# Scaling of one weight split over the two ends of a two-layer attention kernel, and idle matrix products on TensorE in its last batch and last feed-forward

## The chip, the cores and the metric

The kernel runs on one core of a Trainium2 chip. The metric is the device time of one execution in microseconds (us). The engines are TensorE (PE in the profile; PEld are its weight loads), VectorE (DVE), ScalarE (ACT), GpSimd (POOL) and the queue that SyncE (SP) feeds with transfers.

## The reference, cut to what matters

Two layers run over 32 batches of 112 rows with 256 columns; each batch has a context of 375 rows.

```python
x = x + xattn0(layernorm(x), ctx)   # 16 heads of 64
x = x + ffn0(layernorm(x))          # ternary weights, rows quantised to 8 bits, conv over rows, silu
x = x + xattn1(layernorm(x), ctx)   # 16 heads of 16, RMS norm and rotary on q and k
x = x + ffn1(layernorm(x))          # w1, w2 quantised per row; inputs by ONE scale over all batches

def quant_weight_int8_perchannel(w):          # used by ffn1
    s = maximum(max(abs(w), axis=1, keepdims=True), EPS) / 127.0
    return clip(round(w / s), -128.0, 127.0) * s
def quant_act_uint8(x):                       # the maximum is over the whole tensor
    s = maximum(max(x), EPS) / 255.0
    return clip(round(x / s), 0.0, 255.0) * s
```

Since ffn1 takes a maximum over all batches, it can only start when the last batch has left xattn1. A second such maximum, over the hidden values, stands between its two halves.

## The kernel before, in words

**Order.** It is written out by hand for each engine, with semaphores between the engines. All engines run: an opening (weights, batch 0's keys, values and queries, and the first 8 head pairs, `attention(OPENING)`), then a loop of 31 rounds, each `rest(b)` and `attention(MIDDLE, b)`, then `rest(31, True)` and `attention(CLOSING, 31)`, and then ffn1 over 8 groups of 4 batches.

**`rest`.** It ends the first attention of batch b (`wo0_product`, L471), takes the row statistics (`moments`), quantises the rows to `xq` (L1065), turns them on PE (L540), multiplies (L550), runs the convolution on DVE and ACT (L1173, L1185, L854), turns the result (L563), quantises it (L1209, L1210), turns it (L574), multiplies (L588), adds it (L1220), normalises it (L1006), turns it (L597), forms the queries of xattn1 (L605), rotates them on DVE (L1232 to L1239) and turns them (`query_turn`, L478). In a loop round PE works on the next batch's keys and values between these steps (`k0_proj`, `v0_proj`, L339). In the last batch there is no next batch, and nothing stands between them.

**`scales(n, part)`.** This scales the weights of ffn1 on DVE. Weight 0 (`f1w1`, 128x2048 numbers) lies in `stage[1]`, weight 1 in `stage[0]`. Part 0 takes the row maxima and their reciprocals (L1139, L1140, L1142), part 1 multiplies (L1144), part 2 rounds into `wnat[n]` (L1147), which lies in the memory of xattn0's query and output weights and so has to wait for the last batch. Weight 0's three parts stand at the head of `rest(31)`, ahead of the sum `x1` (L1161) in DVE's order. `stage[1]` is free, and `f1w1` is loaded into it, since early in the opening (an issue of SP at 33.4 us).

**`ctx_lo`** (L1449) is POOL's subtraction that gives the low part `cT_lo` of the next batch's context; PE needs it for the third and later products of the next batch's keys. POOL does rotary steps (L1476 to L1482) and the inverse roots of the row statistics (L1444, L1445) in the same queue.

**ffn1.** PE turns the weights (L666), waits for their copies, spreads the global maximum (L670, L672), turns the first rows (L688), and makes the hidden values (L679), of which DVE takes the maxima (L1366). Then the second maximum is spread (L704, L706), the hidden values are made again (L679), ACT applies the ReLU (L968), and the second product follows (L721).

Of the kernel before, what the change touches and what calls it, by code (L numbers as in the profile page):

```python
# [10 lines left out]
ALU = mybir.AluOpType  # L11
# [3 lines left out]
P = 128  # L15
# [37 lines left out]
def xattn_ffn_kernel(nc, A, x3_dram, out):  # L53
# [24 lines left out]
    with ExitStack() as ctx:  # L78
# [254 lines left out]
        def _(pe):  # L333
# [191 lines left out]
            def rest(b, last_batch):  # L525
# [8 lines left out]
                if not last_batch:  # L534
                    k0_terms(0, 4).then_inc(s["k0_ready"], 1)
                    k0_proj(b + 1, range(1, 5), True)

                pe.wait_ge(s["xq_ready"], b + 1)
                for c in range(DC):
                    last = pe.transpose(pt_b0[:, c * T:(c + 1) * T], xq[:, c * P:(c + 1) * P], identb[0:T, 0:T])  # L540
# [13 lines left out]
                if not last_batch:  # L554
                    k0_terms(5, 3).then_inc(s["k0_ready"], 1)
                    k0_proj(b + 1, [6, 7], True)
                    v0_proj(b + 1, [0, 1])
                    pe.wait_ge(s["k0_sb"], b * IC + (IC + 7))
                    v0_terms(2, 0, 4)
                for j in range(FC):  # L560
                    if j % HT == 0:
                        pe.wait_ge(s["y_ready"], b * 2 + (j // HT + 1))
                    last = pe.transpose(pa[0:T, j // HT, (j % HT) * P:(j % HT + 1) * P], th[:, j, :], ident[:])  # L563
                    if j % HT == HT - 1:
                        last.then_inc(s["yT_ready"], 1)
                if not last_batch:
                    x0_transpose(b + 1)
                    v0_terms(2, 4).then_inc(s["v0_ready"], 1)
                    q0_proj(b + 1, 0)
                    q0_proj(b + 1, 1, range(0, 1))  # L570
                for j in range(FC):
                    if j % HT == 0:
                        pe.wait_ge(s["hq_ready"], b * 2 + (j // HT + 1))
                    last = pe.transpose((pt_b0, pt_b1)[j // HT][:, (j % HT) * T:(j % HT + 1) * T],  # L574
                                        hq[:, j * P:(j + 1) * P], identb[0:T, 0:T])
                    if j % HT == HT - 1:
                        last.then_inc(s["hqT_ready"], 1)
# [12 lines left out]
                if not last_batch:  # L590
                    v0_proj(b + 1, [3])
                    q0_proj(b + 1, 1, range(1, HT))
                    v0_terms(4, 0, 2)

                pe.wait_ge(s["xn2_ready"], b + 1)
                for c in range(DC):
# [10 lines left out]
                if not last_batch:  # L607
# [2 lines left out]
                    pe.wait_ge(s["q0_sb"], b * 2 + 4)  # L610
                    scores(1, MIDDLE, b)
                else:
                    query_turn(b)
                    pe.wait_ge(s["x3_ready"], b + 1)
                    pe.wait_ge(s["q1_sb"], b + 1)
                    for i in range(AHEAD):
                        scores(i, CLOSING, b)

            def weight_sum(n):

# [50 lines left out]
            pe.wait_ge(s["g_used"], 2)  # L671
            pe.matmul(pt[:, 1, 0:1], ones[0:1, :], t8[0:1, 1, 0:1], start=True, stop=True).then_inc(s["g_ready"], 1)  # L672
            pe.wait_ge(s["wT_sb"], 4)

            def hidden(c, i, dst):

# [16 lines left out]
            for c in range(NCH):  # L693
                pe.wait_ge(s["xq3T_sb"], c + 2)
                for i in range(4):
# [4 lines left out]
                    if i == 2 and c < NCH - 1:  # L700
                        transpose_rows(c + 1)

            pe.wait_ge(s["g_used"], 3)
            pe.transpose(pt[0:1, 0, 0:P], t8[:, 2, 0:1], ident[:]).then_inc(s["g_ready"], 1)  # L704
            pe.wait_ge(s["g_used"], 4)
# [275 lines left out]
        def _(dve):  # L981
# [105 lines left out]
            def x3_step(n, b):  # L1087
# [13 lines left out]
                else:  # L1101
                    link(dve.tensor_copy(mr[:, bass.ds(b, 1), :].rearrange("p a c -> p (a c)"), st[:, 3, 0:2]))

            def attention(part, b):
                count = G if part == MIDDLE else PAIRS
                k = 0 if part == OPENING else b + 1
# [12 lines left out]
                        turned(i - 1, part, b)  # L1119
                if part != CLOSING:  # L1120
                    k1_squares(k, 0)
                    k1_squares(k, 1)
                turned(count - 1, part, b)
                if part != CLOSING:
# [5 lines left out]
                    for n in range(5):  # L1130
                        x3_step(n, b)

            def scales(n, part):

                w, rows, width = ((stage[1][:], FC, D), (stage[0][:], DC, F))[n]
                by_row = w.rearrange("p (r d) -> p r d", r=rows)
                if part == 0:
                    dve.wait_ge(s["f1w2_in" if n else "f1w1_in"], 16)
                    link(dve.tensor_reduce(t8[:, 8, 0:rows], by_row, AX_X, ALU.max, apply_absolute_value=True))  # L1139
                    link(dve.tensor_scalar(t8[:, 6 + n, 0:rows], t8[:, 8, 0:rows], U8_EPS, 1.0 / 127.0, ALU.max,  # L1140
                                           ALU.mult))
                    link(dve.reciprocal(t8[:, 8, 0:rows], t8[:, 6 + n, 0:rows]))  # L1142
                elif part == 1:
                    link(dve.tensor_tensor(by_row, by_row, t8[:, 8, 0:rows].unsqueeze(2).to_broadcast([P, rows, width]),  # L1144
                                           ALU.mult))
                else:
                    dve.tensor_scalar(wnat[n], w, ROUND, ROUND, ALU.add, ALU.subtract).then_inc(s["dve_end"], 1)  # L1147

            def rest(b, last_batch):
                if not last_batch:  # L1150
                    dve.wait_ge(s["x_in"], b * 16 + 32)
# [1 line left out]
                else:  # L1153

                    dve.tensor_scalar(mr[:, 0:B - 1, 1], mr[:, 0:B - 1, 1], LN_EPS, None, ALU.add)\
                        .then_inc(s["dve_end"], 1)
                    for part in range(3):
                        scales(0, part)
                dve.wait_ge(s["wo_ready"], b + 1)
                dve.wait_ge(s["xbo_ready"], b + 1)  # L1160
                dve.tensor_tensor(x1[:], pa[0:T, 0, 0:D], xbo[:], ALU.add).then_inc(s["x1_ready"], 1)  # L1161
# [131 lines left out]
                row_max(i, OPENING, 0)  # L1293
            row_sum(0, OPENING, 0)
            attention(OPENING, 0)
            with dve.Fori(0, B - 1) as b:
                step.begin(b)
                rest(b, False)
# [316 lines left out]
```

## Time and profile before

| | |
|---|---|
| median of 3 runs | 2430.49 us (2429.35 to 2436.9) |
| the profiled execution | 2424.58 us, of which the trace spans 2422.8 us |
| busy share PE, DVE, ACT, POOL | 96%, 68%, 65%, 68% |
| mean granted TensorE clock | 0.988 of full |
| chain of waits that ended last | PE 85%, ACT 5%, DVE 5%, POOL 2%, issue 3% |
| last batch's `rest` begins (L471) | 2243.97 us |
| ffn1 begins (L666) | 2304.38 us |

The trace counts microseconds from the start of the span. A row of the order of time gives the start, the time that a group of instructions took, the engine, the line, what is written and read, the number of instructions, and in brackets the engine's idle time ahead of the group with what ended it. In the 31 loop rounds PE is busy nearly all the time; from the last batch's `rest` on it is not.

### The profile page before, as it was taken

The numbers are of one execution on the slowest core, as the hardware profiler recorded it, in microseconds if no ns is written. First come the engines' busy times: TensorE is split into PE (matmuls) and PEld (weight loads), VectorE is DVE, ScalarE is ACT, GpSimd is POOL, SyncE is SP. The second block draws the span as 40 slices with busy tenths as digits, with TensorE's granted clock in tenths as the row PEclk, the third lists the DMA queues.
The fourth block names the chain that finished last, engine by engine and source line by source line (L and its number), as shares of the span: only waits on it lengthen the run. The fifth ranks groups of instructions, "written<-read, shape, count | busy, mean of one in ns | idle before, by whom it ended". The sixth has DMA issues, their size and how long they took to land.

```text
span 2422.8 us, 61267 instructions
## 1 busy us (share of the span) xinstructions
PE 2332.0 (96%) x20064; PEld 1764.1 (73%) x20064; DVE 1658.7 (68%) x4412; ACT 1570.3 (65%) x4305; POOL 1646.3 (68%) x1894
## 2 busy tenths in 40 slices
PE   6999999999999999999999999999999999999578
PEld 5777777777777777777777777777777777777336
DVE  6666666776666677666666766666677666666785
ACT  4666666766666676666666766666676666767346
POOL 3766777666668767666776666677667667776507
PEclk9999999999999999999999999999999999999789
DMA  4000000000000000000000000000000000000202
GB/s 161 27 11 10 10 8 10 2 10 10 10 10 8 10 2 10 10 10 10 10 8 5 7 10 10 10 10 8 10 2 10 10 10 10 8 4 0 56 10 62
DMA packets 31197, 37.04 MB, mean 15 GB/s; under 512 B 3284, under 2 KB 29636, under 8 KB 31172
## 3 DMA queue, kind: packets, MB, share of 16 engines
q1 hardware_dynamic: 31172, 36.71, 5.2%
q8 instruction: 15, 0.25, 0.0%
q14 instruction: 10, 0.08, 0.0%
HBM read 29.36 MB, written 7.34 MB: 15 GB/s over the span
## 4 chain that ended last, share of the span: by engine, by line
PE 85%; ACT 5%; DVE 5%; issue 3%; POOL 2%; DMA 0%; ACTq 0%; POOLq 0%; DVEq 0%; SPq 0%
PE ps L339 25%; PE ps L400 15%; PE pt L424 10%; PE pa L436 5%; PE ps L383 5%; PE pa L471 5%; PE pa L451 4%; PE pt L414 4%; ACT prob L790 3%; PE pt L339 2%; PE pa L339 2%; DVE nmx L1025 1%; PE pa L605 1%; PE pa L563 1%; ACT q L830 1%
## 5 line engine op out<-in xcount | busy, mean ns | idle before, releaser
L1025 DVE TENSOR_REDUCE nmx<-ps 112x2 f32<-112x750 f32 x512 | 476.2, 935 | 183.9 <-PE ps L400 177.7
L1462 POOL TENSOR_TENSOR prob<-prob,rinv 112x375 f32<-112x375 f32 x512 | 405.0, 812 | 259.9 <-DVE rinv L1041 256.2
L1462 POOL TENSOR_TENSOR f1w_room<-f1w_room,rinv 112x375 f32<-112x375 f32 x512 | 404.7, 814 | 26.2 <-DVE rinv L1041 22.4
L746 ACT ACTIVATE room<-ps 128x375 f32<-128x375 f32 (+2 forms) x480 | 227.5, 487 | 267.6 <-PE ps L339 267.6
L746 ACT ACTIVATE probT<-pt 125x336 f32<-125x336 f32 (+1 forms) x512 | 242.5, 474 | 138.0 <-PE pt L414 84.1
L1487 POOL TENSOR_TENSOR krs<-krs,nhalf 125x48 f32<-125x48 f32 x32 | 257.1, 8033 | 0.0
L400 PE MATMUL ps<-kT,q 64*112 64x375 f32 x1024 | 227.9, 521 | 11.4 <-ACT prob L790 10.2
L1016 DVE COPY probT<-pt 125x336 f32<-125x336 f32 x322 | 161.8, 502 | 95.9 <-PE pt L424 95.9
L400 PE MATMUL ps<-room,q 64*112 64x375 f32 x1024 | 220.8, 512 | 3.0 <-ACT prob L790 1.9
L790 ACT ACTIVATE prob<-ps,nmx 112x375 f32<-112x375 f32 x256 | 144.7, 576 | 70.2 <-DVE nmx L1025 70.2
L436 PE MATMUL pa<-probT,room 125*64 125x112 f32 x3072 | 182.5, 264 | 0.0
L790 ACT ACTIVATE f1w_room<-ps,nmx,qrs 112x375 f32<-112x375 f32 x256 | 167.9, 663 | 21.9 <-DVE nmx L1033 21.9
L424 PEld LDWEIGHTS pt<-ident,prob 112*125 112x125 f32 x966 | 120.9, 188 | 83.6 <-issue 59.2
L790 ACT ACTIVATE prob<-ps,nmx,qrs 112x375 f32<-112x375 f32 x256 | 169.0, 674 | 17.1 <-DVE nmx L1033 13.5
L424 PEld LDWEIGHTS pt<-ident,f1w_room 112*125 112x125 f32 x966 | 125.0, 187 | 73.2 <-POOL f1w_room L1462 41.0
L436 PEld LDWEIGHTS pa<-probT,room 125*64 125x64 f32 x3072 | 148.2, 136 | 24.8 <-issue 11.0
L424 PE MATMUL pt<-ident,prob 112*125 112x112 f32 x966 | 153.2, 290 | 1.8
L424 PE MATMUL pt<-ident,f1w_room 112*125 112x112 f32 x966 | 146.7, 282 | 6.6 <-DVE probT L1012 1.0
L339 PE MATMUL ps<-cT_hi,wk_lo 128*128 128x376 f32 x512 | 135.7, 346 | 15.1 <-POOL cT_lo L1449 15.1
L790 ACT ACTIVATE f1w_room<-ps,nmx 112x375 f32<-112x375 f32 x256 | 144.6, 577 | 2.5 <-DVE nmx L1025 0.9
L1444 POOL TENSOR_TENSOR st<-st,lneps 112x1 f32<-112x1 f32 x96 | 18.2, 190 | 188.3 <-DVE st L1002 188.3
L1185 DVE SCALAR_TENSOR_TENSOR z<-hp,convw,z 128x112 f32<-128x112 f32 x512 | 138.5, 330 | 3.6
(267 smaller groups left out, 5579.7 us busy)
## 6 DMA issues: line engine op xcount, KB each, us to landing
craw<-in_ctx SPq DMA_DIRECT2D x32, 375.0 KB, 3.1
xin<-in_x SPq DMA_DIRECT2D x32, 112.0 KB, 2.0
x_rows<-x SPq DMA_DIRECT2D x32, 112.0 KB, 1.9
out<-probT SPq DMA_DIRECT2D x16, 224.0 KB, 2.4
room<-x_rows SPq DMA_DIRECT2D x1, 2576.0 KB, 13.3
stage<-in_f1w SPq DMA_DIRECT2D x2, 1024.0 KB, 5.1
stage<-in_wk SPq DMA_DIRECT2D x1, 1024.0 KB, 6.9
stage<-in_wv SPq DMA_DIRECT2D x1, 1024.0 KB, 9.3
```

Of the source, the lines that this page charges most:

```text
L339: last = pe.matmul(dst, left(l, c), right(r, c), start=(n == 0), stop=(n == len(TERMS) - 1))
L383: last = pe.matmul(ps[:, g + 1, j * T:(j + 1) * T], wq0[:, c, (HT * g + j) * P:(HT * g + j + 1) * P], xn0T[:, c, :], start=(c == 0), stop= ...
L400: last = pe.matmul(ps[0:T, 2 * (i % 2) + n, 0:S], q, k, start=True, stop=True)
L424: last = pe.transpose(pt[0:SK, n, t * T:(t + 1) * T], prob(i, n)[:, t * SK:(t + 1) * SK], ident[0:T, 0:T])
L436: last = pe.matmul(pa[r:r + DH0, p // HT, (p % HT) * T:(p % HT + 1) * T], v0[0:SK, t, h * DH0:(h + 1) * DH0], probT[:, 2 * (i % 4) + n, t, :],
L746: return act.activation(dst, src, ACT.Copy)
L790: ins = act.activation(prob(i, n), ps[0:T, 2 * (i % 2) + n, 0:S], ACT.Exp, bias=nmx[:, g:g + 1], scale=scale, accum_out=rsum[:, g:g + 1])
L1016: dve.tensor_copy(probT[:, 2 * (i % 4) + 1, :, :], pt[0:SK, 1, 0:KT * T].rearrange("p (k t) -> p k t", k=KT))\
L1025: top = dve.tensor_reduce(nmx[:, g:g + 2], ps[0:T, 2 * (i % 2):2 * (i % 2) + 2, 0:S], AX_X, ALU.max, negate=True)
L1185: ins = dve.scalar_tensor_tensor(z[:, j, :], hp[:, j, tap:tap + T], convw[:, j, tap:tap + 1], z[:, j, :], ALU.mult, ALU.add)
L1462: pool.tensor_tensor(prob(i, n), prob(i, n), rinv[:, g:g + 1].to_broadcast([T, S]), ALU.mult).then_inc(s["normed"], 1)
L1487: step.link(pool, pool.tensor_tensor(krs[:, 2, :], krs[:, 1, :], nhalf[0:SK, :], ALU.pow))
```

## The change: part of the scaling moved to the opening, and 98 matrix products whose results nobody reads

Parts 0 and 1 of `scales(0, ...)` leave the head of `rest(31)`. Part 0 goes into `attention(OPENING)`, between the squares of the first and the second third of batch 0's keys; part 1 goes behind `attention(OPENING)`, ahead of the loop. Part 2 stays. PE gets a helper `idle_products(count, bank)`: `count` products of 128x128 by 376 columns (f32r) of weights and context that lie in memory, written into a bank that is free. Eight calls are added: 14, 28, 10, 8, 6 and 4 products in the last batch's `rest`, 14 ahead of the first rows of ffn1, 14 ahead of the spread of the second maximum.

The first four pieces of the diff are else-branches in `rest`, at the places where a loop round works on the next batch: after `wo0_product`, ahead of the turn of `th`, ahead of the turn of `hq`, and ahead of the turn of `xn`.

```diff
+                else:
+                    idle_products(14, ps[:, 1, 0:SE])
...
+                else:
+                    idle_products(28, ps[:, 1, 0:SE])
...
+                else:
+                    idle_products(10, ps[:, 1, 0:SE])
...
+                else:
+                    idle_products(8, ps[:, 1, 0:SE])
...
                 else:
+                    idle_products(6, ps[:, 1, 0:SE])
                     query_turn(b)
+                    idle_products(4, ps[:, 1, 0:SE])
                     pe.wait_ge(s["x3_ready"], b + 1)
...
+            def idle_products(count, bank):
+                for _ in range(count):
+                    pe.matmul(bank, wk0[0][:, 0, 0:P], cT[0][:, 0, :], start=True, stop=True)
...
             pe.wait_ge(s["wT_sb"], 4)
+            idle_products(14, ps[:, 1, 0:SE])
...
+            pe.wait_ge(s["xq3T_sb"], NCH + 1)
+            idle_products(14, pa[:, 1, 0:SE])
             pe.wait_ge(s["g_used"], 3)
...
                     k1_squares(k, 0)
+                    if part == OPENING:
+                        scales(0, 0)
                     k1_squares(k, 1)
...
-                    for part in range(3):
-                        scales(0, part)
+                    scales(0, 2)
...
             attention(OPENING, 0)
+            scales(0, 1)
             with dve.Fori(0, B - 1) as b:
```

DVE at the end of the opening, before: the squares of the keys (`krs<-room`) and then the loop's first instruction.

```order
L1056 TENSOR_REDUCE krs<-room 125x16 x2
L1016 COPY probT<-pt 125x336
L1056 TENSOR_REDUCE krs<-room 125x16
L1127 TENSOR_SCALAR krs<-krs 125x48
L1296 UNCONDITIONAL_BRANCH
L1296 ISA
L1000 BN_STATS st<-xin 112x6
```

The same place in the changed kernel (its line numbers are some 20 higher; `t<-stage` is part 0, `stage<-stage,t` part 1).

```order
L1075 TENSOR_REDUCE krs<-room 125x16
L1129 TENSOR_REDUCE t<-stage 128x8
L1130 TENSOR_SCALAR t<-t 128x8
L1132 RECIPROCAL t<-t 128x8
L1075 TENSOR_REDUCE krs<-room 125x16
L1035 COPY probT<-pt 125x336
L1075 TENSOR_REDUCE krs<-room 125x16
L1164 TENSOR_SCALAR krs<-krs 125x48
L1134 TENSOR_TENSOR stage<-stage,t 128x2048
L1317 UNCONDITIONAL_BRANCH
L1317 ISA
L1019 BN_STATS st<-xin 112x6
```

The three instructions of part 0 now stand between the first two squares, and the multiplication over 128x2048 stands ahead of the loop.

DVE at the head of the last batch's `rest`, before: the row scale `mr`, weight 0's five instructions, then the sum `x1` (`x<-pa,xbo`).

```order
L1155 TENSOR_SCALAR mr<-mr 112x31
L1139 TENSOR_REDUCE t<-stage 128x8
L1140 TENSOR_SCALAR t<-t 128x8
L1142 RECIPROCAL t<-t 128x8
L1144 TENSOR_TENSOR stage<-stage,t 128x2048
L1147 TENSOR_SCALAR wqo<-stage 128x2048
L1161 TENSOR_TENSOR x<-pa,xbo 112x256
```

The same place in the changed kernel.

```order
L1176 TENSOR_SCALAR mr<-mr 112x31
L1137 TENSOR_SCALAR wqo<-stage 128x2048
L1181 TENSOR_TENSOR x<-pa,xbo 112x256
L1019 BN_STATS st<-x 112x6
L1015 COPY am<-nhalf 112x1
```

Only the rounding is left ahead of the sum.

PE in the last batch's `rest`, before, from `wo0_product` on.

```order
L471 MATMUL pa<-wqo,oT 112x256 x4
L540 MATMUL pt<-identb,xq 128x112 x2
L543 MATMUL pa<-diag,ones 128x112
L550 MATMUL pt<-xqT,f0w_q 128x112 x16
L563 MATMUL pa<-ident,th 112x128 x8
L574 MATMUL pt<-identb,hq 128x112 x8
L582 MATMUL pa<-ident,room 128x125 x6
L588 MATMUL pt<-f0w_q,hqT 112x256 x8
L597 MATMUL pt<-ident,xn 128x112 x2
```

The same place in the changed kernel; L633 is the helper's product.

```order
L471 MATMUL pa<-wqo,oT 112x256 x4
L633 MATMUL ps<-cT_hi,wk_hi 128x376 x14
L543 MATMUL pt<-identb,xq 128x112 x2
L546 MATMUL pa<-diag,ones 128x112
L553 MATMUL pt<-xqT,f0w_q 128x112 x16
L633 MATMUL ps<-cT_hi,wk_hi 128x376 x28
L568 MATMUL pa<-ident,th 112x128 x8
L633 MATMUL ps<-cT_hi,wk_hi 128x376 x10
L581 MATMUL pt<-identb,hq 128x112 x8
L589 MATMUL pa<-ident,room 128x125 x6
L595 MATMUL pt<-f0w_q,hqT 112x256 x8
L633 MATMUL ps<-cT_hi,wk_hi 128x376 x8
```

Each step of PE that waits for rows of DVE now has a run of such products ahead of it in PE's queue.

## Rows read from the trace of the kernel before

**Rows 1.** Busy time by stretch: PE, PEld, DVE, ACT, POOL; granted clock; DMA.

```profile
2245.95:2250.39 4.44, 0.00 (x1) 0.00 (x0) 4.30 (x5) 0.00 (x0) 0.00 (x0) 1.00 1.10 251
2250.44:2270.92 20.48, 7.71 (x48) 6.73 (x49) 16.12 (x45) 7.48 (x17) 15.45 (x5) 0.50 0.31 68
2274.33:2287.98 13.65, 9.39 (x28) 4.22 (x27) 8.82 (x19) 5.14 (x16) 4.07 (x5) 0.50 0.00 1
2308.46:2318.70 10.24, 5.02 (x21) 2.51 (x22) 5.91 (x23) 5.29 (x10) 0.00 (x0) 0.50 0.12 39
2356.24:2363.07 6.83, 6.43 (x18) 2.54 (x19) 3.80 (x20) 3.34 (x6) 0.00 (x0) 0.50 0.00 0
```

**Rows 2.** Order of time, head of the last batch: PE's L471, DVE up to `x1`.

```profile
2243.97 1.98 PE L471 MATMUL pa<-wqo,oT 128*112 128x256 f32 x8 [0.64 <-ACT oT L746]
...
2244.17 2.28 DVE L1139 TENSOR_REDUCE t<-stage 128x8 f32<-128x2048 f32 x1
...
2249.25 1.23 DVE L1147 TENSOR_SCALAR wqo<-stage 128x2048 bf16<-128x2048 f32 x1
2250.39 0.42 DVE L1161 TENSOR_TENSOR x<-pa,xbo 112x256 f32<-112x256 f32 x1
```

**Rows 3.** Order of time in the opening: DVE beside POOL.

```profile
11.14 2.29 DVE L1269 TENSOR_TENSOR wk_lo<-stage,wk_hi 128x2048 fp32r<-128x2048 f32 x1 [4.75 <-ACT wk_hi L746]
11.90 3.04 POOL L1449 TENSOR_TENSOR cT_lo<-craw,cT_hi 128x750 fp32r<-128x750 f32 x1 [11.45 <-ACT cT_hi L746]
...
62.67 0.42 DVE L1056 TENSOR_REDUCE krs<-room 125x16 f32<-125x256 f32 x1 [3.03 <-ACT v L746]
...
65.48 1.64 POOL L1449 TENSOR_TENSOR cT_lo<-craw,cT_hi 128x750 fp32r<-128x750 f32 x1
65.49 0.42 DVE L1000 BATCH_NORM_STATS2 st<-xin 112x6 f32<-112x256 f32 x1
...
67.44 0.51 PE L339 MATMUL ps<-cT_lo,wk_hi 128*128 128x376 f32 x2
```

**Rows 4.** Order of time: products of 376 and of 448 columns on PE.

```profile
70.23 0.50 PE L339 MATMUL ps<-cT_lo,wk_hi 128*128 128x376 f32 x2
...
70.57 0.51 PE L339 MATMUL ps<-cT_hi,wk_hi 128*128 128x376 f32 x2
...
2357.53 6.01 PE L679 MATMUL ps<-wqo,f1w_room 128*128 128x448 bf16 x16
```

**Rows 5.** Order of time: the same steps in round 1 and in the last batch.

```profile
144.29 0.28 PE L540 MATMUL pt<-identb,xq 112*128 112x112 bf16 x2
...
146.04 1.16 DVE L1173 TENSOR_TENSOR hp<-pt,rb 128x448 f32<-128x448 f32 x2 [1.50 <-PE pt L550]
...
2254.51 0.37 PE L540 MATMUL pt<-identb,xq 112*128 112x112 bf16 x2 [8.56 <-DVE xq L1065]
...
2256.94 1.15 DVE L1173 TENSOR_TENSOR hp<-pt,rb 128x448 f32<-128x448 f32 x2 [2.05 <-PE pt L550]
...
2263.35 1.96 PE L563 MATMUL pa<-ident,th 128*112 128x128 f32 x8 [6.14 <-DVE th L1195]
...
2271.49 0.48 DVE L1220 SCALAR_TENSOR_TENSOR x<-pt,am,x 112x256 f32<-112x256 f32 x1 [0.58 <-PE pt L588]
...
2277.27 0.42 DVE L1232 TENSOR_TENSOR q1b<-pa,ropq 112x256 f32<-112x256 f32 x1 [1.01 <-PE pa L605]
...
2279.94 2.85 PE L400 MATMUL ps<-kT,q 64*112 64x375 f32 x8 [0.76 <-issue]
...
2281.57 0.94 DVE L1025 TENSOR_REDUCE nmx<-ps 112x2 f32<-112x750 f32 x1 [1.20 <-PE ps L400]
```

**Rows 6.** Order of time: the first rows of ffn1, and its second half's start.

```profile
2312.84 0.90 PE L688 MATMUL pa<-identb,hq 112*128 112x112 bf16 x8 [4.11 <-issue]
...
2316.63 1.09 DVE L1366 TENSOR_REDUCE th<-ps 128x2 f32<-128x896 f32 x1 [0.87 <-PE ps L679]
...
2359.30 2.77 ACT L968 ACTIVATE stage<-ps,t 128x448 f32<-128x448 f32 x4 [10.42 <-PE ps L679]
```

More of the change, by code:

```diff
@@ L1102, in x3_step, with scales @@
                     link(dve.tensor_copy(mr[:, bass.ds(b, 1), :].rearrange("p a c -> p (a c)"), st[:, 3, 0:2]))
+            def scales(n, part):
+                w, rows, width = ((stage[1][:], FC, D), (stage[0][:], DC, F))[n]
+                by_row = w.rearrange("p (r d) -> p r d", r=rows)
+                if part == 0:
+                    dve.wait_ge(s["f1w2_in" if n else "f1w1_in"], 16)
+                    link(dve.tensor_reduce(t8[:, 8, 0:rows], by_row, AX_X, ALU.max, apply_absolute_value=True))
+                    link(dve.tensor_scalar(t8[:, 6 + n, 0:rows], t8[:, 8, 0:rows], U8_EPS, 1.0 / 127.0, ALU.max,
+                                           ALU.mult))
+                    link(dve.reciprocal(t8[:, 8, 0:rows], t8[:, 6 + n, 0:rows]))
+                elif part == 1:
+                    link(dve.tensor_tensor(by_row, by_row, t8[:, 8, 0:rows].unsqueeze(2).to_broadcast([P, rows, width]),
+                                           ALU.mult))
+                else:
+                    dve.tensor_scalar(wnat[n], w, ROUND, ROUND, ALU.add, ALU.subtract).then_inc(s["dve_end"], 1)
             def attention(part, b):
@@ L1131, in attention @@
                         x3_step(n, b)
[L1133 to L1147, printed above, removed]
             def rest(b, last_batch):
```

## The prediction

> **What bounds the kernel now.** I read the busy shares first: PE is busy 96% of the span, so over the 31 rounds only PE's own work counts. The change leaves the rounds alone. It touches the end of the opening, the last batch and ffn1, so I read busy time by stretch there [rows 1]. In four stretches, together 20.48 + 13.65 + 10.24 + 6.83 = 51.2 us, the granted clock is 0.50, that is 1.2 GHz; elsewhere it is 1.00, 2.4 GHz. Ahead of the first of them PE had done nothing for 4.4 us, in which the clock was still 1.00. In that stretch PE is busy for 7.71 us of 20.48 while DVE is for 16.12: the last batch is a chain from engine to engine, and its PE steps count at their own length, at half rate. Then I read the order of time at each step of this chain, and in the opening the two queues that the moved work joins, DVE's and POOL's.
>
> **The change part by part.** The sum is made against the profiled execution, 2424.58 us (span 2422.8 us and 1.8 around it). That lies 5.9 us below the median 2430.49; I take the differences over to the median and keep the 5.9 in mind for the range.
>
> *Head of the last batch.* PE's L471 ends at 2243.97 + 1.98 = 2245.95, yet the sum `x1` starts at 2250.39, since DVE first works on weight 0 from 2244.17 to 2250.48 [rows 2]. Of that only the rounding stays, 1.23 us, over at 2245.4. `x1` then waits for PE alone and starts some 0.04 us after it, at 2245.99: **-4.4 us**. Next late is nothing else: POOL and ACT are idle in that stretch [rows 1], and everything up to `xq` hangs on `x1`. The large transfer of rows that runs then feeds ffn1 only, 60 us later.
>
> *Part 0 in the opening.* Its three instructions take 2.28 us [rows 2] and some 0.4 us for the two small ones, 2.7 in all. They go ahead of the second square, before which DVE is idle for 3.03 us until ACT has copied values [rows 3]. The cover holds with 0.3 us to spare, and if it were gone the price would be a few tenths. `f1w1` was asked for at 33 us and is there. Price 0.
>
> *Part 1 in the opening.* Its multiplication takes as long as its twin L1269, 2.29 us, both inputs in SBUF, and starts where `moments` started, at 65.49. POOL's L1449 starts at 65.48 [rows 3]. The same pair met once before: while L1269 ran (to 13.43), L1449 took 3.04 us from 11.90 instead of the 1.64 that it takes at 65.48. So POOL did next to nothing for 1.5 us [rows 3]. In the new place, should DVE be first, L1449 ends 2.3 us later, at some 69.4, where PE has to start its third product at 67.44: +1.9 us on PE's own path. Should POOL be first, I expect DVE to stand until 67.12 and to hold up POOL's next instructions until 69.4. POOL's queue then has the last rotary step and two inverse roots, of which the second is behind `xq`, and PE, which is fed closely there, waits: shifting that queue by 2.29 us and taking off the 0.75 us for which POOL waited for the statistics leaves +1.5. The lower bound is 0, when only instructions of equal kind collide. I take **+1.6 us**, as both orders lie near it, and keep 0 and 2.1. `moments` itself has room: DVE has nothing to do between it and `x1` for over 3 us.
> For the order the Trainium skill has a rule, in "SBUF — State Buffer", section "Who interferes with whom": a VectorE instruction with two SBUF inputs and a GpSimd instruction that reads SBUF exclude each other for the whole of the one that started first. By it the 0 is excluded and the case of POOL first holds, 1.5; the row shows only DVE first. The page also says that a `tensor_reduce` never contends, which would leave part 0 free.
>
> *Price of an idle product.* At 1.00 two products of 376 columns follow each other every 0.34 us, so one takes 0.17 [rows 4]. At 0.50 sixteen of 448 columns take 6.01 us, 0.375 each, so 376 columns take 0.315 (estimate by columns) [rows 4]. If the clock stays at 1.00, the eight blocks take 2.4, 4.8, 1.7, 1.4, 1.0, 0.7, 2.4 and 2.4 us. The gaps of PE that they have to fit into are: 4.1 us for the first (2245.95 to 2250.1); 6.1 us for the second [rows 5]; for the third to sixth about 2.5, 2.8, 1.4 and 0.8, read from the same order of time; for the seventh 4.0 of the 4.11 us ahead of L688 [rows 6]; for the last 3.1. All fit, the sixth just so. They cost nothing by themselves as long as the clock is at 1.00.
>
> *What the clock gives back in the last batch.* If it stays at 1.00: from the turn of `xq` to the first product with the row scale it takes 2256.94 - 2254.51 = 2.43 us; in round 1 it takes 1.75, with three of the next batch's products in between (0.4 us), so 1.35: -1.1. L563 turns eight tiles in 1.96 us; four of them at half the time: -0.5. Before `x2` (L1220) DVE is idle 0.58 us for PE, and before L1232 1.01 us; since weight 1's parts 0 and 1 on DVE end just there, no more than these can be won: -0.5 and -0.9. The turn of the queries: -0.2. The closing scores: eight products in 2.85 us, twice, of which the chain waits for the first four each time; half of 1.4 us, twice: -1.3 (DVE is idle 1.20 us ahead of its maximum, so there is room) [rows 5]. Together **-4.6 us**. POOL does not become late: its long power instructions hang on DVE's steps, which move with it.
>
> *First rows of ffn1.* The clock falls here at 2308.46, before the wait that the seventh block stands behind is over, so I expect its fourteen products at 0.315: 4.4 us against 4.0, +0.4. They bring the clock up earlier; DVE waits 0.87 us and then 0.33 for the first hidden values, and would not: -1.2. Together with a shorter L688 I take **-0.7 us**, from +0.4 to -1.4 [rows 6].
>
> *Second half of ffn1.* With the clock kept, the first hidden values take half of 2359.30 - 2357.53 = 1.77 us, -0.9, and the two small products of the spread another 0.2: **-1.1 us** [rows 4, 6].
>
> The sum is -4.4 + 1.6 - 4.6 - 0.7 - 1.1 = **-9.2 us**: 2430.49 - 9.2 = 2421.3 (2415.4 on the profiled execution).
>
> **The rivals.** (a) *The blocks leave one gap too wide.* After the first block PE is still idle for 1.7 us, after the fourth for 2; the clock fell once although the stretch had started with PE at work (2274.33, soon after L588). If it falls behind the fourth block, the 0.9, 0.2 and 1.3 are lost, and the fifth and sixth blocks are 0.5 late each: 3.4 less, 2424.7. Behind the first block it is some 1.8. Taken as 2424.5.
> (b) *The products get no higher clock, and are in nobody's way.* Then only the move is left, -4.4 + 1.6 = -2.8: 2427.7. The change would not do what it says. Against it: the clock rose each time during a dense run of products.
> (c) *The opening costs nothing*: -10.8, 2419.7.
> (d) *The products themselves become the wait, at 1.2 GHz.* Then the blocks take 4.4, 8.8, 3.2, 2.5, 1.9, 1.3, 4.4 and 4.4 us against the gaps above: 0.3 + 2.7 + 0.7 + 0 + 0.5 + 0.5 + 0.4 + 1.3 = 6.4 late, -2.8 + 6.4 = +3.6: 2434.1, slower. The place is the second block; it decides from the point where the clock is at 0.50 for more than eight of its 28 products (28 x 0.17 + 8 x 0.145 = 6.0). Against it: such a run brings the clock up by itself.
>
> **How the numbers follow.** The forecast has 0.45, (a) 0.26, (b) 0.10, (c) 0.12, (d) 0.07. A measurement of this kernel tells about 0.3%, 7.3 us, from no change. Faster by more than that are most of the forecast (0.36), nearly all of (c) (0.11) and a third of (a) (0.09): 0.56. Slower by it is only a much worse (d): 0.04. The rest, 0.40, is within. The range goes from 2414.5, the forecast with two thirds of the distance to the profiled execution, a little beyond it for (c), to 2428, which takes in (a) and (b) and leaves out (d).
>
> **What would show it.** In the changed profile: `x1` starts 0.04 us after L471's end in the last batch (the move is right); L1449 in the first `rest` or the multiplication in the opening takes far longer than 1.64 or 2.29 us, and round 1 starts some 1.6 us later; the granted clock between `x1` and the closing attention stays 1.00; `th` is turned at once when DVE has it, not after products. It is wrong if the clock falls in the last batch all the same, if products delay a turn, or if what PE gives back is taken up by DVE's scaling of weight 1.

## The result, and the profile after

| | before | after |
|---|---|---|
| median of 5 runs | 2430.49 us (2429.07 to 2436.9) | 2420.01 us (2418.05 to 2422.4) |
| ratio after/before | | 0.9959, 95% interval 0.9945 to 0.9973 |
| profiled execution, its span | 2424.58, 2422.8 us | 2421.54, 2419.7 us |
| mean granted TensorE clock | 0.988 | 0.996 |

The medians are 10.5 us apart; the forecast had 9.2 us and 2421.3. The two profiled executions are only 3.0 us apart, since that of before lies 5.9 us below its median and that of after 1.5 us above its own. What is compared row by row below is therefore compared with an unusually short execution of before; a second execution of before (`c_before`, further down) shows what was unusual in it.

The order of time of after, the end of the opening (the same place as [rows 3]; lines are some 20 higher than before):

```profile
60.87 2.28 DVE L1129 TENSOR_REDUCE t<-stage 128x8 f32<-128x2048 f32 x1
...
64.05 0.42 DVE L1075 TENSOR_REDUCE krs<-room 125x16 f32<-125x256 f32 x1 [0.38 <-ACT v L765]
...
66.88 3.78 POOL L1470 TENSOR_TENSOR cT_lo<-craw,cT_hi 128x750 fp32r<-128x750 f32 x1
66.88 2.28 DVE L1134 TENSOR_TENSOR stage<-stage,t 128x2048 f32<-128x2048 f32 x1
...
70.71 0.61 PE L339 MATMUL ps<-cT_lo,wk_hi 128*128 128x376 f32 x2 [1.79 <-POOL cT_lo L1470]
```

Part 0 is hidden: the square behind it still waits 0.38 us for ACT. Part 1 is not. It begins in the same hundredth as POOL's subtraction `cT_lo`, which now takes 3.78 us in place of 1.64, and PE waits 1.79 us for it.

The head of the last batch [rows 2], and the steps that [rows 5] shows of before:

```profile
2247.94 1.98 PE L471 MATMUL pa<-wqo,oT 128*112 128x256 f32 x8 [0.64 <-ACT oT L765]
...
2248.14 1.22 DVE L1137 TENSOR_SCALAR wqo<-stage 128x2048 bf16<-128x2048 f32 x1
...
2249.96 0.42 DVE L1181 TENSOR_TENSOR x<-pa,xbo 112x256 f32<-112x256 f32 x1 [0.60 <-PE pa L471]
...
2254.09 0.27 PE L543 MATMUL pt<-identb,xq 112*128 112x112 bf16 x2 [1.77 <-DVE xq L1084]
...
2255.73 1.29 DVE L1193 TENSOR_TENSOR hp<-pt,rb 128x448 f32<-128x448 f32 x2 [1.26 <-PE pt L553]
...
2256.13 6.08 PE L633 MATMUL ps<-cT_hi,wk_hi 128*128 128x376 f32 x28
...
2262.15 1.38 PE L568 MATMUL pa<-ident,th 128*112 128x128 f32 x8
...
2269.23 0.48 DVE L1240 SCALAR_TENSOR_TENSOR x<-pt,am,x 112x256 f32<-112x256 f32 x1
...
2275.00 0.42 DVE L1252 TENSOR_TENSOR q1b<-pa,ropq 112x256 f32<-112x256 f32 x1 [0.99 <-PE pa L614]
...
2278.37 0.94 DVE L1044 TENSOR_REDUCE nmx<-ps 112x2 f32<-112x750 f32 x1 [0.49 <-PE ps L400]
...
2281.17 0.89 PE L400 MATMUL ps<-kT,q 64*112 64x375 f32 x4 [2.21 <-ACT prob L809]
```

`x1` follows L471's end by 0.04 us. The 28 products of the second block end with the gap. And PE stands idle for 2.21 us in the closing attention, at a place that no block fills.

Busy time by stretch of after; the columns are those of [rows 1], the last but two is the granted clock:

```profile
2250.00:2255.00 5.00, 3.07 (x22) 2.60 (x21) 3.25 (x12) 0.36 (x1) 3.72 (x3) 1.00 1.10 253
2255.00:2258.80 3.80, 3.80 (x26) 3.80 (x24) 2.91 (x8) 2.67 (x8) 3.80 (x1) 0.55 1.13 279
2272.50:2275.80 3.30, 2.93 (x9) 2.52 (x10) 2.27 (x4) 0.23 (x1) 0.00 (x0) 0.55 0.00 0
2282.70:2292.70 10.00, 10.00 (x63) 6.52 (x65) 6.26 (x19) 6.89 (x19) 8.29 (x11) 0.51 0.00 0
```

In the last batch of before the clock was at 0.50 for 34 us [rows 1]; here for about 17, in three pieces. Each begins within 1.2 us of the end of a gap of PE: 1.77 us ahead of L543, 2.18 ahead of the turn of `xn` (L606), 2.21 in the closing attention.

The first rows of ffn1 and the start of its second half [rows 6]:

```profile
2308.14 2.67 PE L633 MATMUL ps<-cT_hi,wk_hi 128*128 128x376 f32 x14 [0.19 <-ACT f1w_room L765]
...
2312.02 0.57 PE L705 MATMUL pa<-identb,hq 112*128 112x112 bf16 x8 [1.21 <-DVE hq L1383]
...
2315.03 2.09 DVE L1387 TENSOR_REDUCE th<-ps 128x2 f32<-128x896 f32 x2
...
2354.25 0.27 PE L723 MATMUL pt<-ident,t 128*1 128x128 f32 x1 [0.75 <-DVE t L1413]
...
2356.23 4.42 ACT L987 ACTIVATE stage<-ps,t 128x448 f32<-128x448 f32 x7 [9.37 <-PE ps L696]
```

The seventh block ran at 1.00 and delayed nothing. L723 is the turn of the second maximum; the same turn in before:

```profile
2356.27 0.37 PE L704 MATMUL pt<-ident,t 128*1 128x128 f32 x1 [3.15 <-DVE t L1392]
```

### The profile page after: what moved, and what is told of

Its sections match the earlier page's. It is cut to its first block, busy times and chain, and to the rows that moved or that the text cites. A ratio compares the mean times of both kernels' runs of the same rounds, so it can differ in the third digit from the quotient of the medians.

```text
span 2419.7 us, 61464 instructions
## 1 busy us (share of the span) xinstructions
PE 2344.5 (97%) x20162; PEld 1778.6 (74%) x20162; DVE 1659.9 (69%) x4412; ACT 1572.5 (65%) x4305; POOL 1650.4 (68%) x1894
## 4 chain that ended last, share of the span: by engine, by line
PE 84%; ACT 5%; DVE 5%; issue 3%; POOL 2%; DMA 0%; POOLq 0%; ACTq 0%; DVEq 0%; SPq 0%
PE ps L339 24%; PE ps L400 15%; PE pt L424 10%; PE pa L436 5%; PE ps L383 5%; PE pa L471 5%; PE pa L451 4%; PE pt L414 4%; ACT prob L809 3%; PE pt L339 2%; PE pa L339 2%; DVE nmx L1044 1%; PE pa L614 1%; PE pa L568 1%; ACT q L849 1%
## 5 line engine op out<-in xcount | busy, mean ns | idle before, releaser
L1483 POOL TENSOR_TENSOR f1w_room<-f1w_room,rinv 112x375 f32<-112x375 f32 x512 | 405.2, 815 | 25.8 <-DVE rinv L1060 22.1
```

Of the source, the lines that this page charges most:

```text
L1483: pool.tensor_tensor(prob(i, n), prob(i, n), rinv[:, g:g + 1].to_broadcast([T, S]), ALU.mult).then_inc(s["normed"], 1)
```

## The experiments

Since start-up alone differs by up to 2.6 us between executions (the first score product of the opening starts at 37.65 us in one trace and at 40.28 in another), each trace is read from the end of the last batch's L471 on. The table has the start of some steps, in us from there, each from the order of time of the kernel named in the row; the clock is the granted clock of the 60 us behind L471's end.

| kernel | `x1` | `hp` | turn of `th` | `x2` | first closing maximum | ffn1 begins | end of span | clock |
|---|---|---|---|---|---|---|---|---|
| before | 4.44 | 10.99 | 17.40 | 25.54 | 35.62 | 58.43 | 176.85 | 0.72 |
| `c_before` | 4.44 | 11.00 | 17.41 | 25.86 | 36.09 | 62.08 | 180.33 | 0.60 |
| `move_only` | 0.04 | 6.23 | 12.64 | 21.10 | 31.33 | 57.14 | 175.38 | 0.63 |
| `idle_only` | 4.44 | 10.99 | 17.65 | 24.68 | 33.87 | 59.32 | 176.21 | 0.80 |
| after | 0.04 | 5.81 | 12.23 | 19.31 | 28.45 | 53.75 | 169.78 | 0.86 |
| `after_again` | 0.04 | 5.59 | 12.01 | 19.09 | 27.26 | 51.13 | 167.20 | 0.91 |
| `closing_only` | 0.04 | 5.59 | 12.02 | 19.09 | 27.27 | 49.37 | 165.36 | 0.97 |
| `both_again` | 0.03 | 5.58 | 11.99 | 19.07 | 27.25 | 49.36 | 166.24 | 0.99 |
| `open_fill` | 0.04 | 5.58 | 12.00 | 19.08 | 27.26 | 49.36 | 166.27 | 0.99 |

**The theory** was that the change saves the 4.4 us in front of `x1` and a second part by the clock, and pays 1.6 us in the opening. The rivals were that only one half of it works.

**The two halves alone.** `move_only` is after without its eight calls; `idle_only` is before with them.

```diff
# move_only, against after: the helper does nothing
             def idle_products(count, bank):
-                for _ in range(count):
-                    pe.matmul(bank, wk0[0][:, 0, 0:P], cT[0][:, 0, :], start=True, stop=True)
+                pass
...
# idle_only, against after: the scaling as before
-                    if part == OPENING:
-                        scales(0, 0)
...
-                    scales(0, 2)
+                    for part in range(3):
+                        scales(0, part)
...
-            scales(0, 1)
```

> The changed kernel without its 98 idle products; the scaling stays moved. Theory A (the clock is what the products buy, the move is worth its 4.4 us less what it costs in the opening): x1 of the last batch starts 0.04 us after L471's end, the granted clock falls in the last batch, before the first rows of ffn1 and before its second half as in the kernel before, PE waits 1.8 us for cT_lo once in the opening; 2430.5 - 4.4 + 2.0 = 2428.1 us, ratio 0.999. Rival (the timed gain is mostly the move, the profile of before being a low one): 2422 to 2424, ratio 0.997.

> The kernel before with the 98 idle products alone; the three parts of weight 0's scaling stand at the head of the last batch again. Theory A: no wait for cT_lo beyond the usual in the opening; x1 starts 4.4 us after L471's end, and the 14 products of the first block end 2 us before it, so that the clock falls there. From the last batch's L471 to the end it gains what the products gave in the changed kernel (7.0 - 4.4 = 2.6 us) or up to 4.6 where the clock happens to hold: 2426 to 2428 us. Rival (products need the move to work at all): within 1 us of before.

> The changed kernel once more, on the same chip as the others. Ratio 0.996 as before. If the clock falls in the last batch depend on where the gaps lie in time and not on the code, the second profile shows them at other places: after the fourth block or in the closing attention in some executions and not in others. If they are fixed by the code, they are at the same two places (behind the fourth block, and in the third scores of the closing attention).

Measured, beside 2429.77 for before on that chip: `move_only` 2427.53 (ratio 0.9991, 0.9982 to 1.0001), `idle_only` 2424.87 (0.9979, 0.997 to 0.9987), `after_again` 2421.45 (0.9969, 0.9959 to 0.9979). So the move is worth 2.2 us by medians, the products 4.9 (7.1 in all), and both together 8.3. The interval of `move_only` just takes in no change. `idle_only` gained more than the 2426 to 2428 us expected. `after_again` has low clock at 2279.8 to 2286.7 and at 2303.7 to 2307.2: again in the closing attention, but not behind the first or the fourth block, so neither of the two readings expected of it holds alone.

In `idle_only` the products were also once in the way. `x1` still comes late, and the clock is low from 2253.7 to 2263.9. PE's order of time there:

```profile
2260.12 6.79 PE L633 MATMUL ps<-cT_hi,wk_hi 128*128 128x376 f32 x28
2266.74 1.14 PE L568 MATMUL pa<-ident,th 128*112 128x128 f32 x8
```

The 28 products take 6.79 us and no idle time is left ahead of L568, which comes 0.25 us later than in before (17.65 against 17.40 in the table). As long as the clock is low they follow each other every 0.31 us (the forecast's estimate was 0.315). This is rival (d) where it was expected, in the second block with more than eight products at 1.2 GHz, at a quarter of a microsecond, paid back by `x2`.

**Why POOL's subtraction waits.** `reduce_there` has a reduction with one input over the same memory where after has part 1, and leaves part 1 at the head of the last batch.

```diff
+                    scales(0, 1)
                     scales(0, 2)
...
             attention(OPENING, 0)
-            scales(0, 1)
+            link(dve.tensor_reduce(t8[:, 9, 0:FC], stage[1][:].rearrange("p (r d) -> p r d", r=FC), AX_X, ALU.max,
+                                   apply_absolute_value=True))
```

> A reduction of the same 128x2048 numbers (one input in SBUF, 2.28 us) stands in the opening where part 1 stood, and part 1 stands at the head of the last batch again. Theory P (two SBUF inputs on DVE shut POOL out): L1449's subtraction takes 1.64 us, PE does not wait for cT_lo beyond 0.2 us, and x1 of the last batch starts 2.0 us after L471's end, +1.96. Rival (any long DVE instruction there delays the next batch, by DVE's queue or by memory): the subtraction takes 3.8 us or PE waits 1.8 us as with part 1.

```profile
67.76 1.64 POOL L1472 TENSOR_TENSOR cT_lo<-craw,cT_hi 128x750 fp32r<-128x750 f32 x1
67.77 2.27 DVE L1317 TENSOR_REDUCE t<-stage 128x8 f32<-128x2048 f32 x1
```

The order of time shows the same place, the same memory and the same length on DVE, and POOL takes 1.64 us: it is the kind of the instruction that shuts POOL out, not a busy DVE. The reduction has one input where the multiplication has two, and it also writes only 128x8 numbers, so this run does not tell the second input from the long output. The Trainium skill has the rule in "SBUF — State Buffer", section "Who interferes with whom" (a VectorE instruction with two SBUF inputs excludes a GpSimd instruction that reads SBUF, a `tensor_reduce` never contends); both rows agree. They do not bear out an order that goes by the start in the rows, as the forecast took it from the Trainium skill: in `closing_only` POOL stands at 68.88 and DVE at 68.89, and POOL waited all the same. The single time was 2419.09 us; `x1` comes 1.67 us after L471's end here, so the opening's wait is exchanged for a nearly equal one.

One input is no safeguard either. The opening of before has, in a place that the change leaves alone, a DVE instruction with one input over 128x2048, first without and then beside a POOL instruction:

```profile
29.58 1.23 DVE L1082 TENSOR_SCALAR stage<-stage 128x2048 f32<-128x2048 f32 x1
...
49.39 2.56 POOL L1462 TENSOR_TENSOR prob<-prob,rinv 112x375 f32<-112x375 f32 x2
49.48 1.81 DVE L1082 TENSOR_SCALAR stage<-stage 128x2048 f32<-128x2048 f32 x1
```

It takes 1.81 us in place of 1.23, and POOL's two products 2.56 in place of the 1.58 that such a pair takes elsewhere in the opening.

`act_scale` takes both prices away: ScalarE does part 1 as eight copies with a scale per partition, at the head of the last batch, once DVE's reciprocal of part 0 has signalled `row8`, and part 2 goes from there to behind the closing attention.

```diff
+                else:
+                    act.wait_ge(s["row8"], 1)
+                    for r in range(FC):
+                        w = stage[1][:, r * D:(r + 1) * D]
+                        ins = act.activation(w, w, ACT.Copy, scale=t8[:, 8, r:r + 1])
+                    ins.then_inc(s["mul8"], 1)
...
-                    scales(0, 2)
...
+                    dve.wait_ge(s["mul8"], 1)
...
-            scales(0, 1)
...
+            scales(0, 2)
```

> The kernel after, but part 1 of the scaling is done by ScalarE in eight pieces at the head of the last batch, beside the attention there, and VectorE does only its two reciprocals and the rounding of the part. Theory (the third term of the keys in the opening waits 1.8 to 2.0 us because VectorE's part 1 and GpSimd's round begin together): that wait is gone and the round takes 1.64 us again, x1 follows the end of the last attention product by 0.04 us still, and the time is 1.8 to 2.0 us below that of the kernel after, 2419.5 on the chip of the earlier runs. Rival (ScalarE's pieces hold up the attention of the last batch, or VectorE's rounding behind them comes late for x1): the time is that of the kernel after or above it, with x1 more than 1 us behind the last attention product.

Measured: 2419.38, beside 2430.68 for before (ratio 0.9951, 0.9938 to 0.9965).

```profile
68.44 1.64 POOL L1479 TENSOR_TENSOR cT_lo<-craw,cT_hi 128x750 fp32r<-128x750 f32 x1
70.40 0.51 PE L339 MATMUL ps<-cT_lo,wk_hi 128*128 128x376 f32 x2
...
2247.18 3.29 ACT L867 ACTIVATE stage<-stage,t 128x256 f32<-128x256 f32 x8
...
2247.34 1.98 PE L471 MATMUL pa<-wqo,oT 128*112 128x256 f32 x8 [0.64 <-ACT oT L765]
...
2249.36 0.42 DVE L1189 TENSOR_TENSOR x<-pa,xbo 112x256 f32<-112x256 f32 x1 [1.73 <-PE pa L471]
```

The wait is gone (POOL's start to PE's product is 1.96 us, as before the change; 3.83 in after), and `x1` is not late: 1.87 us, as the theory has it, in the trace. By medians it gained only 0.0008 to 0.0018 of the ratio against the two measurements of after (1.8 to 2.0 us were expected), which their intervals don't tell from nothing. Its profile shows part of the reason. It has a stretch of low clock from 44 to 51 us in the opening, which after's profiles have not (from the first score product there to POOL's `cT_lo` it takes 28.77 us, in after 27.54), and one of 13.7 us in the closing attention (10.2 in after); from L471's end to the end it takes 170.78 us, 1.0 more than in after.

**Where the clock is still lost.** `more` lengthens the first and the fourth block and adds two; `closing_only` adds to after one block alone, behind the first two closing scores.

```diff
# more, against after
-                    idle_products(14, ps[:, 1, 0:SE])
+                    idle_products(22, ps[:, 1, 0:SE])
...
-                    idle_products(8, ps[:, 1, 0:SE])
+                    idle_products(19, ps[:, 1, 0:SE])
...
# more and closing_only, against after
                     for i in range(AHEAD):
                         scores(i, CLOSING, b)
+                    idle_products(12, pt[:, 1, 0:SE])
...
# more, against after: ahead of the spread of the first maximum
+            idle_products(7, pa[:, 0, 0:SE])
```

> The kernel after with more idle products: 22 in place of 14 in the first block of the last batch, 19 in place of 8 in the fourth, and two new blocks, 12 behind the first two score products of the closing attention and 7 ahead of the first feed-forward. Theory (what the kernel after still loses in the last batch is a lower granted clock behind gaps that no product or too few fill, the fourth block and the closing attention): the granted clock stands at 1.00 through most of the last batch and the time is 1.5 to 3 us below that of the kernel after, about 2419. Rival (the new blocks end after the rows that the next products wait for, above all where the clock is already down and a block lasts twice as long): the rows wait for TensorE, the time is equal or up to 3 us above that of the kernel after.

> The kernel after with one more block of 12 idle products, behind the first two score products of the closing attention, and nothing else. Theory (the gap of some 2 us there is where most of the clock is still lost, 2.5 us in the profiled execution of after): this block alone brings 1 to 2.5 us against the kernel after, and the granted clock stands at 1.00 from the block to the last feed-forward. Rival (what the four new or longer blocks brought together was the first and the fourth block's share): the time is that of the kernel after within 0.5 us, and low clock is seen behind the fourth block or the closing attention as before.

Measured: `more` 2418.69 (before 2430.68; 0.9952, 0.9939 to 0.9966); `closing_only` 2419.21 (before 2430.57; 0.9957, 0.9943 to 0.997). Busy time of the 20 us from the third closing score on, after first, `closing_only` second:

```profile
2281.17:2301.17 20.00, 18.33 (x158) 12.35 (x158) 11.79 (x34) 12.90 (x36) 14.52 (x18) 0.74 0.00 1
```

```profile
2281.81:2301.81 20.00, 16.37 (x200) 11.31 (x200) 13.28 (x37) 12.88 (x38) 14.40 (x18) 1.00 0.00 1
```

With the block the clock is 1.00 and PE gets through 200 products in place of 158. From the first closing maximum to ffn1 it takes 22.10 us, in after 25.30 and in `after_again` 23.87. `more` reaches ffn1 at 49.37 too: what the longer first and fourth blocks add cannot be seen beside `closing_only`, whose clock did not fall there in its traced execution. The six traces with this block (also `both`, `both_again`, `open_fill`, `block2_42`) all take 22.1 us there. The eight without it take 22.5 to 26.2: `reduce_there` 22.47, before 22.81, `act_scale` 26.16. So the block is worth 0.4 to 4.1 us by the traces, as the clock happens to fall without it; by medians the gain over after is not resolved.

**Both, and a block in the opening.** `both` is `act_scale` with `more`. `open_fill` adds eight products to it in the opening, at a place that the change never touched.

```diff
             for i in range(AHEAD):
                 scores(i, OPENING, 0)
+            idle_products(8, pt[:, 1, 0:SE])
             attention(OPENING, 0)
```

> Both edits of the two kernels before it. Theory (they act at different places, the opening and the last batch): the savings add, 3.5 to 5 us below the kernel after, about 2417. Rival (one of them is worth nothing): the time of the better one of the two.

> The kernel with both edits once more, beside the one with the block in the opening. Theory (its execution does not differ from one look to the next by more than its runs, 2413 to 2420 us): the ratio to the kernel before lies in 0.993 to 0.9956, and the last attention product to the end takes 168.5 us of the span within 1.5. Rival (its median was a lucky one): a ratio of 0.996, that of the kernel after.

> The kernel with both edits, and 8 idle products more in the opening, behind the first two score products of batch 0, at a place that the change itself leaves alone: TensorE stands idle there for 1.7 us, and in the traces of eight changed kernels the granted clock fell to 0.50 behind it for 3 to 12 us, while in four (twice the kernel before, twice after) it did not. Theory (that gap is what lets the clock fall, and the fall costs what these eight lose): the granted clock stays at 1.00 from 40 to 60 us, the distance from the first score product of the opening to the start of POOL's part cT_lo is 27.5 us in place of 28.3, and the time is 0.5 to 2 us below that of both edits. Rival (the fall comes for another reason, or the gap is too short to matter): low clock is seen there as before, and the time is the same within 0.5 us.

Measured: `both` 2417.44 (before 2430.68; 0.9942, 0.9929 to 0.9956), `both_again` 2420.0 (before 2430.01; 0.9953, 0.9939 to 0.9967), `open_fill` on the same chip as the latter 2416.75 (0.9946, 0.9933 to 0.996). The 168.5 us expected of `both_again` were counted from L471's start; so counted it takes 168.26 (166.24 from its end). `open_fill` and `both_again` were timed beside the same runs of before, and `open_fill` is 3.2 us below by medians, more than the 0.5 to 2 expected; the intervals overlap. The traces show what the block does: `both_again` first, `open_fill` second, 20 us from just behind the first score product on.

```profile
40.00:60.00 20.00, 18.02 (x131) 12.49 (x129) 14.71 (x23) 11.68 (x39) 11.92 (x14) 0.74 0.01 2
```

```profile
38.00:58.00 20.00, 17.30 (x148) 12.06 (x145) 17.40 (x26) 13.36 (x43) 14.49 (x15) 1.00 0.01 2
```

From the first score product to POOL's `cT_lo` it takes 30.28 us in `both_again` (39.73 to 70.01) and 27.43 in `open_fill` (37.67 to 65.10): 2.85 us, of code that is the same but for the block. The clock fell at this place, for 3 to 10 us, in the nine profiles of the other changed kernels and in none of the four of before, `c_before`, after and `after_again`; by the same distance the fall cost 0 (`move_only`) to 2.8 us (`closing_only`); why it spared those four stays open, since what runs ahead of it is the same in all. `open_fill` has the lowest median of the study, 13.3 us below before, but is not told apart from `both`, which lay 13.2 us below before on its own chip (ratio 0.9942 against 0.9946).

**A block that is too long.** `block2_42` is `both` with 42 products in the second block.

```diff
-                    idle_products(28, ps[:, 1, 0:SE])
+                    idle_products(42, ps[:, 1, 0:SE])
```

> The kernel with both edits (the part on ScalarE and more idle products), with 42 idle products in place of 28 in the second block, whose gap the 28 leave 1.3 us of. Theory (an idle product costs 0.17 us at clock 1.00, and beyond the gap all of it is in the way): the 14 more take 2.4 us, TensorE no longer waits at the product behind them, and this one comes 1.1 us later than with 28, counted from the first idle product; the stretch from the last attention product to the end is 169.6 us in place of 168.5. Rival (VectorE or a wait elsewhere takes the lateness up): the stretch is 168.5 within 0.3 us.

```profile
2255.47 7.46 PE L634 MATMUL ps<-cT_hi,wk_hi 128*128 128x376 f32 x42
2262.77 1.03 PE L568 MATMUL pa<-ident,th 128*112 128x128 f32 x8
```

The 28 of `both` take 5.06 us, so fourteen more take 2.40, 0.171 each. The turn of `th` comes at 12.99 from L471's end in place of 11.99: 1.00 us late (1.1 expected), and `x2` 0.94. The stretch to the end is 167.12 against 166.57 in `both`, +0.55, and against 166.24 in `both_again`, +0.88; ffn1 begins 0.93 later than in the latter. Each of the three has one stretch of low clock of 3.4 us in ffn1; here and in `both_again` it begins 10 us behind ffn1's start, in `both` 16 us. So the nearer comparison is +0.88, and little of the lateness is taken up. The one time was 2418.71 us.

**Before once more.**

> The kernel before once more, unchanged. Theory (the granted clock falls at other places from one execution to the next, in the opening too): the last attention product ends at 2244 to 2250 us of the span, and the stretch from it to the end takes 178 to 180 us. Rival (each kernel has its own places of low clock): the rows of the profiled execution of before come back within 0.3 us, the last attention product at 2243.97.

Measured: 2429.75 us, near the median of before. L471 ends at 2247.57, 1.62 us later than in the first profile, and from there to the end it takes 180.33 us in place of 176.85 (178 to 180 expected). Nearly all of this comes between the first closing maximum and ffn1 (+3.2): here the clock stays low from 2251.3 to 2299.1.

```profile
2251.66:2300.00 48.34, 28.05 (x150) 18.56 (x152) 32.53 (x84) 18.68 (x50) 27.97 (x21) 0.51 0.17 42
```

In the first profile it was back at 1.00 from 2270.92 to 2274.33 and again from 2287.98 on [rows 1]. That is 3.5 of the 5.9 us by which the profiled execution was below its median. The 53 timed executions of before beside the experiments go the same way: the twelve below 2428 us have a mean granted clock of 0.987 to 0.989, the seventeen above 2431 us one of 0.983 to 0.986.

## Why the prediction was right, and where not

- **Head of the last batch, -4.4.** Exact: `x1` at 0.04 from L471's end in place of 4.44, and `xq`'s turn at 4.17 in place of 8.56. Nothing else became late.
- **Part 0, 0.** Right; the cover left 0.38 us (0.3 said).
- **Part 1, +1.6.** Right in mechanism and nearly in size: DVE had the right of way, the case that the forecast priced at +1.9; the 1.5 that it took from the order of starts did not come. From POOL's start to PE's third product it takes 3.83 in place of 1.96 us, +1.87, and round 1 (L543) stands 1.99 further from its start-up (147.59 against 144.29 is 3.30 later, of which 1.31 had arisen by 57 us). Rival (c) is excluded.
- **Price of an idle product.** 0.171 at 1.00 (0.17 said) and 0.31 at 0.50 (0.315 said).
- **The clock in the last batch, -4.6.** Half of the closing scores' 1.3 lies behind the first closing maximum, so the forecast has -3.95 between `x1` and that maximum (the terms that it lists add up to 4.5, not 4.6, and to 3.85 here). Before takes 31.18 us there, after 28.41, -2.8; `after_again`, whose clock stayed at 1.00 up to there, 27.22, -3.96. So the sizes of the steps hold and the clock did not: rival (a), at both places that it named, behind the first block (low from 2255.0 to 2258.4) and behind the fourth (2272.1 to 2275.5). Step by step in after: `hp` gave 0.8 (1.1 said), the turn of `th` nothing, `x2` 1.06 behind it (1.0 said for the two turns), the rotary product nothing (0.9 said), the queries and the first scores 0.9 (0.85 said). By the forecast's own sign ("it is wrong if the clock falls in the last batch all the same") this part of it failed in the profiled execution, and held in `after_again` up to the first closing maximum.
- **What the step left out** is what comes behind: the forecast took only the first closing scores and ended its sum with them, while the closing attention has a gap of its own. In after the clock fell behind it and stayed low for 10 us; from the first maximum to ffn1 it took 25.30 us, 2.5 more than in before (22.81), where the clock had come back early. In `c_before` it took 25.99. Filling this gap (`closing_only`) brings 22.10.
- **First rows of ffn1, -0.7.** The seventh block was expected at 0.50 and 0.4 late; it ran at 1.00 (2.67 us). From ffn1's start to the first hidden maximum: 11.36 in place of 12.25, -0.9. (The forecast's pieces, +0.4, -1.2 and a shorter L688, add up to more than its -0.7.) Part of this is chance too: after has no low clock in ffn1's first 20 us, while the other ten traces of kernels with the block still have one fall of 3.4 us there.
- **Second half, -1.1.** From the turn of the second maximum to the first ReLU: 1.98 in place of 3.03, -1.05. In all eleven traces with the eighth block the clock stays at 1.00 here; the three without it (before, `c_before`, `move_only`) fall for 6.8 us.
- **The sum.** Against the profile of before, -7.1 from L471's end and +1.9 in the opening, that is some -5.2; the other 2.1 of the 3.97 us by which L471 begins later are start-up and small differences of the rounds. Against `c_before` the same stretch gives -10.6, less 1.9: -8.7. The forecast's -9.2 was set against a lucky execution, in which it was 4 us too large; taken over to the medians (-10.5; -8.3 on a second chip) it came out right because the usual execution of before loses more to the clock than its profile showed. That the two nearly cancel is luck; the mechanism holds, its size on the profiled execution did not. The forecast had the 5.9 us only as a distance to keep in the range, not as a clock that had come back early.
- **Readings of the forecast.** At 11.90 POOL lost 3.04 - 1.64 = 1.40 us, not 1.5. The fall of the clock at 2274.33, which the forecast puts soon after L588, came 2.9 us after L588's end and 0.2 us after L597 had begun, behind a gap of 2.75 us, as in the three falls of after. The lower end of the range, 2414.5, is not two thirds of the distance but 0.9 us beyond all of it. None of these changes the forecast.
- **Rivals.** (a) happened in part (behind the first and the fourth block, 3.4 us at 1.2 GHz each) and is one of several forms the same code takes: `after_again` has neither. (b) is out by `idle_only`. (d) showed as a quarter of a microsecond in `idle_only` and as 1.00 us with the 42 products of `block2_42`.

## What to carry to other kernels

Where TensorE works by steps at the end of a kernel, look for every gap (here from 1.7 us up) up to the last dense stretch, not only for those beside the change, and fill each with somewhat fewer products than fit at full clock; a product more than fits costs up to its own 0.17 us on the path. An instruction moved beside another engine's has to be looked at by its kind and inputs, not only by whether its own engine is free: a reduction there was free, a two-input multiplication cost 1.9 us, and ScalarE, which had room at the head of the last batch, took it with `x1` still 0.04 us behind L471. And before a forecast is set against one traced execution, the low-clock stretches of that execution should be taken as one draw: the same code was at 1.2 GHz for 34 us of its last batch in one execution and for 48 in another.

## What the runs showed of the hardware that was not expected

- The stretches of low clock (1.2 GHz) of the same code lie at different places from one execution to the next. In before the clock came back once at 2270.92 and once not before 2299.1; in the opening it fell behind one and the same gap of 1.7 us in nine profiles and not in four, and stayed low for 3 to 10 us.
- PE need not have been idle for long: in after the clock fell 0.2 to 1.2 us behind the end of gaps of 1.77, 2.18 and 2.21 us, with products running again. With eight products (1.64 us in all) in the opening's gap of 1.73 us it did not fall (`open_fill`, one trace).
- When a two-input DVE instruction and POOL's subtraction start within a hundredth of a microsecond of each other, DVE had the right of way each time (66.88, and again in `after_again`, `move_only`, `more` and `closing_only`, each with 3.78 us for POOL and 2.28 for DVE), also in `closing_only`, where POOL's row stands a hundredth earlier.
